# TensorE's instruction order inside an attention slot: row-maximum products behind the slot's other work, value products ahead of it

## The chip, the cores and the metric

The kernel runs on one core of a Trainium2 chip. The metric is the device time in microseconds of one execution; lower is better. The five engines of the core (TensorE, VectorE, ScalarE, GpSimd, SyncE) each run their own instruction list in order and meet only at semaphores.

## The reference

Input is x with 16 sequences of 256 rows and 128 columns. One transformer layer is computed, with 16 heads of 8 columns and 14 experts:

```
qkv = x @ w_qkv ; q, k, v split into 16 heads of 8
scores = q k^T / sqrt(8), causal
out = softmax(scores) @ v
a = layernorm(out @ w_proj + b_proj + x) * gamma + beta
x = layernorm(x + a)
logits = x @ gate_w.T ; the two best of 14 experts, softmax weights
h = gelu(x @ w1[e] + b1[e]) @ w2[e] + b2[e]
x = layernorm(x + clip(x + w_a h_a + w_b h_b, -100, 100))
```

## The kernel before

The program has three stretches. The first, up to about 300 us, is attention with everything that the routing needs, in a software pipeline over slots t = 0 to 21. The second runs the experts on tiles of 128 rows, the first of them already inside the last slots. The third gathers, adds, normalises and stores. The change lies in the first.

A slot t works on several sequences at once, each at another stage: sequence t is transposed and projected (`turn_x`, `project`, the value projection), t-2 gets its row maxima (`maxima` on TensorE, `reduce` on VectorE), t-3 and t-4 get scores, exponentials and value products (`scores`, `values`), t-4 its head normalisation and output projection, t-5 its layer norms and gate, t-6 its ranks and the scatter of its rows. Every slot has eight units u = 0 to 7, and all five engines run the same units, each in the order in which the Python body writes them. No planner moves anything: the order of TensorE's queue is the order of the `if` blocks in its `body`.

Names that matter:

- `maxima(t, r, i)`, i = 0 to 5: a first pass of score products of sequence t-2 into the PSUM tile M (both banks of it), with masks (L1506, L1512). It waits until VectorE has read M for the piece before (`m_reduced`).
- `reduce(i)` on VectorE (L1202): the maxima of one such piece, M into `row_max`. M is a single buffer, so `maxima(i+1)` and `reduce(i)` exclude each other.
- `scores` (L1473, masks L1481) into S[0] or S[1]; ScalarE's exponentials of it (L862) into `probs`.
- `values(t, r, s, k)`, k = 0 to 3 (L1531): probabilities times values of four heads into O, at u = 2, 3 (of t-4) and u = 5, 7 (of t-3).
- `heads_t` copies on ScalarE (L896 after u = 3, L938 after u = 7), `turn_heads` (L1539), then on VectorE `invert_sums` and `normalise_heads` (L1211, L1217).
- `split` on VectorE (L1034), then `m_split` on ScalarE (L882): remainders of the projected rows, for the three bf16 parts. ScalarE issues L882 ahead of L896.
- At u = 6 the transposes `x2T` (L1707) into M[0], which wait until all six reductions of the slot are done, and `on_turned` (L1712). At u = 7 the turn of the row maxima (L1609) into M[1], the gate (L1615) into M[0], the output projection (L1681), and the small product `shift_left` (L1688), which waits for ScalarE's copy L920.
- VectorE at the end of the slot: top two experts (MAX8 L1315, L1318, L1320), `y` (L1327), `both` (L1332); the next slot begins with the statistics of y (L1227) and `reduce(0)`.
- GpSimd scatters the rows of t-6 in units 2 to 5 (L775), from t = 6 on.

The core of VectorE's queue in a slot is: statistics of y, reduce(0), reduce(1), reduce(2), `ys`, `split`, reduce(3), statistics of ys, reduce(4), reduce(5), head normalisation, gate work.

Of the kernel before, what the change touches and what calls it, by code (L numbers as in the profile page):

```python
# [13 lines left out]
P = 128  # L14
# [12 lines left out]
def transformer_layer(nc, x, w_qkv, w_proj, b_proj, ln_gamma, ln_beta, gate_w, w1, b1, w2, b2, out):  # L27
# [49 lines left out]
    def on(s):  # L77

        return not isinstance(s, int) or 0 <= s < B
# [12 lines left out]
    with ExitStack() as ctx:  # L92
# [891 lines left out]
        def _(dve):  # L984
# [182 lines left out]
            def body(t, r, lap):  # L1167
# [128 lines left out]
                reduce(4)  # L1296
                if on(t - 4):
                    invert_sums(0)
                if on(t - 4):
                    normalise_heads(0)  # L1300
                steps(t, 4)
                reduce(5)
                if on(t - 4):
                    invert_sums(1)
                if on(t - 4):
                    normalise_heads(1)
                if t == B + 1:
                    first_list()
# [148 lines left out]
        def _(pe):  # L1457
# [139 lines left out]
            def body(t, r, lap):  # L1597
                for u in range(NP):
# [13 lines left out]
                    if u == 7 and on(t - 5):  # L1612
                        pe.wait_ge(x2T_copied, t - 4)
                        for i in range(TT):
                            last = pe.matmul(M[0][:, T + i * E:T + i * E + E], x2T[:, (r - 5) % R, i * P:i * P + P], gate_t[:, :],  # L1615
                                             start=True, stop=True)
                        last.then_inc(gate_ready, 1)
# [36 lines left out]
                    if u < NM and on(t - 2):  # L1654
                        maxima(t, r, u)
# [19 lines left out]
                    if u == 5 and on(t - 4):  # L1675
                        pe.wait_ge(o_normed, 2 * (t - 4) + 1)
                        turn_heads(t, 1)
                    if u == 7 and on(t - 4):
# [11 lines left out]
                    if pv_quad(t, u) and on(pv_quad(t, u)[0]):  # L1690
                        if u == 2 and on(t - 6):

                            pe.wait_ge(rank_read, t - 5)
                            if t == B + 1:
                                pe.wait_ge(first_table, 1)
                        if u == 5 and on(t):

                            pe.wait_ge(v_copied, t + 1)
                        values(t, r, *pv_quad(t, u))
# [9 lines left out]
                    if u == 6 and on(t - 4):  # L1709
                        pe.wait_ge(o_normed, 2 * (t - 3))  # L1710
                        for i in range(TT):
                            last = pe.transpose(G[:, i * P:i * P + P], heads[:, i], ident[:, :])  # L1712
                        last.then_inc(on_turned, 1)
                    if t == FIRST and u == 2:
# [88 lines left out]
```

## Time and profile before

| what | value |
|---|---|
| median of 3 runs | 504.61 us (498.4 to 506.06) |
| the profiled execution | 504.69 us |
| its span in the trace | 502.9 us |
| granted TensorE clock, mean | 0.886 |
| busy: TensorE, VectorE, GpSimd, ScalarE | 379.2, 325.1, 290.3, 266.8 us |
| reductions of the row maxima (L1202) | 96, the first at 16.7 us, the last at 280.0 us |

The time is that of the core's whole execution; the span is what the trace covers of it. Busy times are sums over instructions of an engine, so an engine can be the bound of one stretch and idle in another. Times in rows are us from the start of the span.

### The profile page before, as it was taken

To read this page: it belongs to the slowest core of one execution; us is meant where nothing else is said; L and a number is where in the kernel's file an instruction comes from. 1 tells how busy PE (TensorE), PEld (TensorE's weight loads), DVE (VectorE), ACT (ScalarE), POOL (GpSimd) and SP (SyncE) were. 2 spreads that over 40 slices of the span, in tenths; PEclk is the share of its full clock that TensorE was granted. 3 is DMA by queue.
4 is the path that set the end of the run, shared out by engine and by line. 5 is a ranking of instruction groups with operands and counts; after the bars stand their busy time and mean duration, and the time that the engine had idled before them with its cause. 6 is when DMAs were issued, how large, how long until landed. Compare 5 with 4: busy or idle time off the path is not lost. (4 is left out here: it accounts for less than half of the span.)

```text
span 502.9 us, 12961 instructions
## 1 busy us (share of the span) xinstructions
PE 379.2 (75%) x4207; PEld 276.0 (55%) x4207; DVE 325.1 (65%) x1053; ACT 266.8 (53%) x624; POOL 290.3 (58%) x454
## 2 busy tenths in 40 slices
PE   5477988977988798879877867765577877777780
PEld 3244555655555555556544435765466867756580
DVE  6634687758777877786786846734444776663386
ACT  2124666756776577666645637443346544444054
POOL 6402346775777668666754365785554555556271
PEclk9556999989999899998989869978787989798996
DMA  5412333334334433442311141222332222220573
GB/s 137 106 52 65 85 101 98 103 87 110 101 91 107 110 84 90 118 113 66 89 50 55 42 68 28 64 69 63 94 108 67 70 69 75 71 69 21 169 230 105
DMA packets 72974, 44.02 MB, mean 88 GB/s; under 512 B 13233, under 2 KB 68931, under 8 KB 72796
## 3 DMA queue, kind: packets, MB, share of 16 engines
q1 hardware_dynamic: 66650, 33.11, 25.0%
q0 software_dynamic: 4640, 9.36, 5.7%
q10 hardware_dynamic: 1618, 0.73, 0.6%
q8 instruction: 34, 0.56, 0.5%
q14 instruction: 32, 0.26, 0.2%
HBM read 18.54 MB, written 12.36 MB: 61 GB/s over the span
## 5 line engine op out<-in xcount | busy, mean ns | idle before, releaser
L1202 DVE TENSOR_REDUCE row_max<-M 128x4 f32<-128x1024 f32 (+1 forms) x96 | 117.2, 1221 | 48.8 <-PE M L1512 37.3
L862 ACT ACTIVATE probs<-S 128x768 f32<-128x768 f32 x128 | 102.7, 816 | 58.3 <-PE S L1481 42.5
L729 POOL DMA_INDIRECT results<-tile_rows x77 | 77.2, 1002 | 57.0 <-DVE tile_rows L1074 37.4
L775 POOL DMA_INDIRECT sorted_rows<-x,row_no x64 | 65.7, 1027 | 33.5 <-DVE row_no L1234 21.0
L1506 PE MATMUL M<-k_stack,q_stack 64*128 64x128 bf16 (+1 forms) x512 | 41.7, 267 | 43.4 <-DVE row_max L1202 40.3
L1531 PE MATMUL O<-probs,diag 128*32 128x256 f32 (+1 forms) x1024 | 58.5, 349 | 3.1 <-DVE row_chosen L1251 3.1
L748 POOL TENSOR_SCALAR_AFFINE_SELECT probs<-probs 128x256 f32<-128x256 f32 x104 | 40.0, 409 | 23.3 <-ACT probs L862 23.2
L1506 PEld LDWEIGHTS M<-k_stack,q_stack 64*128 64x128 bf16 x512 | 16.7, 100 | 62.6 <-DVE row_max L1202 57.0
L1473 PE MATMUL S<-q_stack,k_stack 64*128 64x256 bf16 (+1 forms) x512 | 45.6, 260 | 0.0
L1531 PEld LDWEIGHTS O<-probs,diag 128*32 128x32 f32 x1024 | 27.7, 113 | 25.4 <-issue 9.3
L852 ACT ACTIVATE hT<-S,q_stack 128x128 f32<-128x128 f32 x78 | 25.7, 371 | 25.0 <-PE S L1577 16.0
L782 POOL TENSOR_TENSOR diag<-rest,diag 128x512 bf16<-128x512 f32 x16 | 18.5, 1155 | 35.5 <-ACT diag L882 24.7
L852 ACT ACTIVATE hT<-S,k_stack 128x128 f32<-128x128 f32 x76 | 24.8, 371 | 20.5 <-PE S L1577 9.7
L1577 PE MATMUL S<-rows_t,k_stack 128*128 128x128 f32 x152 | 28.3, 318 | 7.7 <-ACT hT L852 4.4
L1512 PE MATMUL M<-ident_fold,mask_m 64*128 64x128 bf16 (+1 forms) x384 | 33.1, 255 | 0.0
L1577 PE MATMUL S<-rows_t,q_stack 128*128 128x128 f32 x156 | 27.1, 301 | 4.4 <-issue 2.7
L1577 PEld LDWEIGHTS S<-rows_t,k_stack 128*128 128x128 f32 x152 | 24.7, 231 | 8.9 <-issue 8.9
L1584 PE MATMUL M<-k_stack,hT 128*128 128x128 f32 x132 | 24.5, 317 | 4.1 <-DVE tile_rows L1074 3.5
L1473 PEld LDWEIGHTS S<-q_stack,k_stack 64*128 64x128 bf16 x512 | 16.6, 97 | 19.4 <-issue 17.1
L1065 DVE COPY q_stack<-experts 128x642 f32 x39 | 21.7, 559 | 8.0 <-issue 5.0
L1577 PEld LDWEIGHTS S<-rows_t,q_stack 128*128 128x128 f32 x156 | 23.4, 215 | 5.4 <-issue 5.3
L1584 PE MATMUL M<-q_stack,hT 128*128 128x128 f32 x116 | 21.9, 319 | 5.1 <-DVE tile_rows L1074 5.0
(261 smaller groups left out, 861.5 us busy)
## 6 DMA issues: line engine op xcount, KB each, us to landing
q_stack<-diag SPq DMA_DIRECT2D x96, 64.0 KB
k_stack<-diag SPq DMA_DIRECT2D x85, 64.0 KB
tile_rows<-sorted_rows SPq DMA_DIRECT2D x77, 64.5 KB
experts<-in_L_ffn_w_dram SPq DMA_DIRECT2D x28, 128.0 KB
xin<-in_L_attn_target_dram SPq DMA_DIRECT2D x16, 128.0 KB, 3.0
xres<-in_L_attn_target_dram SPq DMA_DIRECT2D x16, 128.0 KB, 3.1
out_dram<-probs SPq DMA_DIRECT2D x8, 256.0 KB, 2.3
q_stack<-results SPq DMA_DIRECT2D x7, 256.0 KB, 3.2
```

Of the source, the lines that this page charges most:

```text
L729: pool.indirect_dma_start(results, bass.IndirectOffsetOnAxis(ap=y_rows[:, slot, D:ROW].bitcast(U32), axis=0), y_rows[:, slot, 0:D], None, ...
L748: last = pool.affine_select(out=diag, in_=diag, compare_op=ALU.is_ge, fill=0.0, base=0, pattern=[[0, 2], [1, P]], channel_multiplier=-1)
L775: pool.indirect_dma_start(sorted_rows, bass.IndirectOffsetOnAxis(ap=row_no[:, q * 2 * TT + n:q * 2 * TT + n + 1], axis=0), x2[:, q, n % 2, ...
L852: act.activation(hT[:, (s - 2) % HR, f], hidden_of(s - 2, f), ACT.Gelu, bias=expert_now[(s - 2) % XR][:, AT_B1 + f:AT_B1 + f + 1]).then_in ...
L862: act.activation(probs[:, n].rearrange("p (a q) -> p a q", a=2), S[n % 2][:, :].rearrange("p (a q) -> p a q", a=2)[:, :, 0:T + P], ACT.Exp ...
L1202: dve.tensor_reduce(row_max[:, (r - 2) % R, :, g0:g0 + ng, half], M_both[:, :].rearrange("p (a h k) -> p a h k", a=2, h=ng), X, ALU.max).t ...
L1473: last = pe.matmul(S[n % 2][:, 512 * a + at:512 * a + at + nq], k_stack[rows, b, n, half * P:half * P + P], q_stack[rows, b, n, T - nq:T], ...
L1506: pe.matmul(M[a][:, j * keys:j * keys + keys], q_stack[rows, b, g0 + j, half * P:half * P + P], k_stack[rows, b, g0 + j, 0:keys], start=(j ...
L1512: last = pe.matmul(diag, mask_m[rows, c], ident_fold[rows, None, :].broadcast_to([TILE, ng, TILE]), start=False, stop=(c == 1), skip_group ...
L1531: last = pe.matmul(O[32 * j:32 * j + 32, at + T - nq:at + T], v_aug[:, b, half, h], probs[:, h // 2, (h % 2) * (T + P) + of:(h % 2) * (T + ...
L1577: pe.matmul(hidden_of(s - 2, f), expert_now[(s - 2) % XR][:, f * P:f * P + P], rows_t[:, (s - 2) % HR], start=True, stop=True).then_inc(h_ ...
L1584: last = pe.matmul(second(s - 4), hT[:, (s - 4) % HR, f], expert_now[(s - 4) % XR][:, AT_W2 + f * D:AT_W2 + f * D + D], start=(f == 0), st ...
```

## The change

On TensorE, three things move inside a unit. `maxima(t, r, u)` for u = 0 to 5 goes from the middle of the unit to its end: behind the projection (u = 2), the turns of the heads and the value projection (u = 4), the second turn (u = 5) and `values`. `values` goes ahead of the output projection, `shift_left`, the gate and the u = 6 transposes; at u = 7 it now stands directly behind the turn of the row maxima. The gate goes from ahead of all this to behind `values`. On VectorE, reduce(4) and reduce(5) each move behind one half of the head normalisation, so that VectorE's order fits TensorE's. No instruction is added or removed, and sizes, buffers and DMAs stay.

```diff
@@ VectorE's body @@
                 steps(t, 3)
-                reduce(4)
                 if on(t - 4):
                     invert_sums(0)
                 if on(t - 4):
                     normalise_heads(0)
+                reduce(4)
                 steps(t, 4)
-                reduce(5)
                 if on(t - 4):
                     invert_sums(1)
                 if on(t - 4):
                     normalise_heads(1)
+                reduce(5)
@@ TensorE's body @@
                         last.then_inc(shift_turned, 1)
-                    if u == 7 and on(t - 5):
-                        pe.wait_ge(x2T_copied, t - 4)
-                        for i in range(TT):
-                            last = pe.matmul(M[0][:, T + i * E:T + i * E + E], x2T[:, (r - 5) % R, i * P:i * P + P], gate_t[:, :],
-                                             start=True, stop=True)
-                        last.then_inc(gate_ready, 1)
...
                         turn_x(t, r, lap)
-                    if u < NM and on(t - 2):
-                        maxima(t, r, u)
...
                         turn_heads(t, 1)
+                    if pv_quad(t, u) and on(pv_quad(t, u)[0]):
+                        if u == 2 and on(t - 6):
+                            pe.wait_ge(rank_read, t - 5)
+                            if t == B + 1:
+                                pe.wait_ge(first_table, 1)
+                        if u == 5 and on(t):
+                            pe.wait_ge(v_copied, t + 1)
+                        values(t, r, *pv_quad(t, u))
+                    if u == 7 and on(t - 5):
+                        pe.wait_ge(x2T_copied, t - 4)
+                        for i in range(TT):
+                            last = pe.matmul(M[0][:, T + i * E:T + i * E + E], x2T[:, (r - 5) % R, i * P:i * P + P], gate_t[:, :],
+                                             start=True, stop=True)
+                        last.then_inc(gate_ready, 1)
...
-                    if pv_quad(t, u) and on(pv_quad(t, u)[0]):
-                        if u == 2 and on(t - 6):
-                            pe.wait_ge(rank_read, t - 5)
-                            if t == B + 1:
-                                pe.wait_ge(first_table, 1)
-                        if u == 5 and on(t):
-                            pe.wait_ge(v_copied, t + 1)
-                        values(t, r, *pv_quad(t, u))
...
                         last.then_inc(on_turned, 1)
+                    if u < NM and on(t - 2):
+                        maxima(t, r, u)
```

## Rows read from the trace of the kernel before

**Rows 1.** The page's groups by line: reductions, products for maxima; busy, mean, idle before.

```profile
L1202 DVE TENSOR_REDUCE row_max<-M 128x4 f32<-128x1024 f32 (+1 forms) x96 | 117.2, 1221 | 48.8 <-PE M L1512 37.3
...
L1506 PE MATMUL M<-k_stack,q_stack 64*128 64x128 bf16 (+1 forms) x512 | 41.7, 267 | 43.4 <-DVE row_max L1202 40.3
```

**Rows 2.** Windows: slot 5; slots 6 to 15; slot 13; slot 14. Columns: length, busy by engine, clock.

```profile
64.71:80.06 15.35, 13.90 (x209) 8.96 (x207) 12.22 (x32) 11.41 (x24) 7.89 (x17) 1.00 0.35 95
80.06:251.68 171.62, 146.00 (x2082) 94.70 (x2077) 127.44 (x354) 114.53 (x222) 121.53 (x220) 0.96 0.36 99
198.93:215.83 16.90, 13.99 (x213) 9.04 (x209) 12.64 (x36) 11.39 (x24) 12.15 (x23) 1.00 0.37 102
215.83:235.33 19.50, 16.68 (x213) 10.80 (x209) 12.75 (x36) 11.48 (x24) 12.60 (x24) 0.82 0.33 88
```

**Rows 3.** Timeline of slot 13, first half: start, length, engine, line, idle before.

```profile
198.93 1.22 DVE L1202 TENSOR_REDUCE row_max<-M 128x4 f32<-128x1024 f32 x1 [0.24 <-PE M L1512]
...
200.21 0.39 PE L1506 MATMUL M<-k_stack,q_stack 64*128 64x256 bf16 x4 [0.58 <-DVE row_max L1202]
...
200.92 1.13 PE L1558 MATMUL G<-diag,wqk 128*128 128x256 f32 x4
...
202.58 0.86 PE L1531 MATMUL O<-probs,diag 128*32 128x256 f32 x16
202.69 1.22 DVE L1202 TENSOR_REDUCE row_max<-M 128x8 f32<-128x1024 f32 x1
...
203.37 0.34 PE L1473 MATMUL S<-q_stack,k_stack 64*128 64x256 bf16 x4
...
204.20 0.28 PE L1512 MATMUL M<-ident_fold,mask_m 64*128 64x128 bf16 x4
...
204.36 0.68 DVE L1034 TENSOR_TENSOR rest<-G,diag 128x512 f32<-128x512 f32 x1
...
205.07 0.62 ACT L882 CAST diag<-rest 128x512 bf16<-128x512 f32 x1 [0.23 <-issue]
...
206.47 1.23 DVE L1202 TENSOR_REDUCE row_max<-M 128x4 f32<-128x1024 f32 x1 [1.43 <-remote]
206.63 0.59 ACT L896 COPY heads_t<-O 128x512 f32<-128x512 f32 x1 [0.94 <-PE O L1531]
...
207.75 0.39 PE L1506 MATMUL M<-k_stack,q_stack 64*128 64x256 bf16 x4 [2.10 <-DVE row_max L1202]
```

**Rows 4.** Timeline of the same slot, second half.

```profile
208.18 0.66 PE L1539 MATMUL G<-ident,heads_t 128*128 128x128 f32 x4
...
209.22 0.34 PE L1473 MATMUL S<-q_stack,k_stack 64*128 64x256 bf16 x4
...
209.63 0.40 PE L1506 MATMUL M<-k_stack,q_stack 64*128 64x128 bf16 x8
...
210.18 0.66 PE L1539 MATMUL G<-ident,heads_t 128*128 128x128 f32 x4
210.29 1.23 DVE L1202 TENSOR_REDUCE row_max<-M 128x8 f32<-128x1024 f32 x1 [0.23 <-PE M L1512]
...
210.76 0.86 PE L1531 MATMUL O<-probs,diag 128*32 128x256 f32 x16
...
211.82 0.44 PE L1707 MATMUL M<-ident,x 128*128 128x128 f32 x2
...
213.06 0.62 PE L1615 MATMUL M<-gate_t,x2T 128*128 128x14 f32 x4
...
213.71 0.26 DVE L1315 MAX8 top_v_all<-M 128x8 f32<-128x14 f32 x2 [1.71 <-PE M L1615]
...
215.10 0.49 DVE L1227 BATCH_NORM_STATS2 stats<-y 128x6 f32<-128x128 f32 x2
```

**Rows 5.** Timeline of slot 5 on VectorE: its third and fourth reductions, no scatter yet.

```profile
68.48 1.22 DVE L1202 TENSOR_REDUCE row_max<-M 128x8 f32<-128x1024 f32 x1 [0.19 <-PE M L1512]
...
70.75 1.21 DVE L1202 TENSOR_REDUCE row_max<-M 128x4 f32<-128x1024 f32 x1
```

## The prediction

> **What bounds the kernel now.** I read the page's groups first. The largest is VectorE's reduction of the row maxima, 96 times 1.22 us; TensorE in turn stands idle 43.4 us ahead of the products that fill M for it, nearly all of it on those reductions [rows 1]. That is 0.45 us per piece and 2.7 us per slot, and it is TensorE's largest wait in the page's groups. So the slot is a shuttle between two engines over one buffer: products, reduction, products. Whatever TensorE is given between two pieces is free up to the 1.22 us of the reduction and is paid beyond it.
>
> The windows say how tight this is. Slot 13 lasts 16.90 us, with TensorE busy 13.99 and VectorE 12.64 [rows 2]. Slots 6 to 15 average 17.16 us at a clock of 0.96. Slot 14, at 0.82, took 19.50: 2.6 more than slot 13 for 0.18 of clock, so 0.04 costs an estimated 0.6 and an average slot at full clock 16.56 us. Slot 5, the last without the scatters of GpSimd (7.89 us busy there against 12.15), took 15.35 [rows 2].
>
> The timeline shows where that difference sits. In slot 13 the products of the fourth piece end at 204.48, and VectorE is free at 205.04, but the reduction starts at 206.47, released late; ScalarE gets the end of the value products only at 206.63; TensorE's next products then stand until 207.75, idle 2.10 [rows 3]. In slot 5 the fourth reduction follows the third after 2.27 us without any wait [rows 5]; in slot 13 after 3.78 [rows 3]. So 1.43 us of a slot goes to a TensorE signal that arrives late near the scatters. Why it is late, these rows don't show.
>
> **The change, as gaps.** No work is added. What changes is what lies between `maxima(i)` and `maxima(i+1)`. Behind piece 0: two scores, rank, turn, as before. Behind piece 1: scores and projection, and now also the values of u = 2. Behind 2: scores and values, as before. Behind 3: scores, the turn of the heads and the value projection, in place of values and scores. Behind 4: scores, second turn, values. Behind 5: one scores, and then the x2T transposes, which need that last reduction. Before, a turn, values and a scores covered it. One gap becomes too full, one empty, and one now hangs on ScalarE.
>
> **One slot walked.** Zero is the start of the products of piece 5 (209.63 before). Distances are between starts in slot 13.
>
> 1. The reduction starts 0.66 later and takes 1.23 [rows 4]; VectorE's end reaches TensorE in 0.06 (200.15 to 200.21 [rows 3]). x2T starts at 1.95. Before it was 2.19, with a turn and values inside [rows 4]; now TensorE idles about 1.1.
> 2. From x2T to the gate it was 1.24 [rows 4]. The values now stand ahead of the gate, 0.79 (202.58 to 203.37 [rows 3]): gate at 3.98. No cover exists for this: VectorE already waits 1.71 for the gate [rows 4].
> 3. Gate to MAX8 0.65, MAX8 to the end of the statistics of y 1.88 [rows 4]: next slot's reduction 0 at 6.51, before at 6.20 (215.83 [rows 2]). Plus 0.31. `shift_left` and its copies on ScalarE come later too, behind values, gate and projection, but TensorE reaches them near 5.2, and `maxima(0)` needs them only about 5.9, so I cost that at nothing; if ScalarE is later than that, it is paid in full.
> 4. Reduction 0 to projection 1.99; the projection 1.13, values 0.79 [rows 3], then `maxima(2)` and 0.66: reduction 2 at 11.08. That is 4.57 after reduction 0, before 3.76 [rows 3]. Plus 0.81.
> 5. Reduction 2 to the end of `split` 2.35, to the end of ScalarE's `m_split` (L882) 3.00, then the copy of the heads (L896) 0.59 [rows 3] and a hand-over at either end: turn of the heads at 14.8. In the old order `maxima(4)` stood ahead of this turn; now it stands behind it, and behind the value projection, 1.04 together [rows 4]: `maxima(4)` at 15.8. Counted from reduction 0 that is 9.3, before 8.82 (198.93 to 207.75 [rows 3]). This is plus 0.48 in all for steps 4 and 5, although the old 8.82 holds the 1.43 of the late signal. What was lost to lateness is now lost to a chain VectorE, ScalarE, TensorE.
> 6. `maxima(4)` 0.43 [rows 3, 4], scores 0.41, second turn 0.58, values 0.79 [rows 3, 4]: `maxima(5)` at 18.02. Before 1.88 for this, now 2.21: plus 0.33. The head normalisation moved ahead of the reduction on VectorE is hidden under the products.
>
> The slot is 18.02 against 16.90, plus 1.12. One term is soft: TensorE's own end is modelled, and behind a 1.13 us projection the next issue may come 0.2 earlier; I take 17.8. Against the full-clock average of 16.56 that is plus 1.25 (bounds 0.9 and 1.5).
>
> The late signal is the unknown. Its old end was 7.54 after reduction 0; at the same distance it would be 14.05, just where ScalarE is free for the copy, so it costs nothing. That is one end. The other is that it follows the products: `maxima(3)` would end at 12.9, and 1.99 later (204.48 to 206.47 [rows 3]) is 14.9, which moves the copy by 0.8 to 0.9 per slot. It could also vanish, and below nothing it can't go, since the chain of step 5 stands without it. I take nothing, as the scatters are issued by GpSimd's clock and not by TensorE's.
>
> **The sum.** Slots 6 to 15: 10 x 1.25 = 12.5. Slot 5 has the same chains and no lateness to trade, 17.8 minus 15.35 [rows 2]: 2.5. Slots 16 and 17 have no projection, split or value projection; steps 1 to 3 and half of 6 remain, about 0.5 each (0 to 1): 1.0. Slots 2 to 4 have neither gate nor x2T and partly a clock at half speed; 0.8 once for step 4 (0 to 2). Slots from 18 on have no maxima; the gate of slot 18 is later by one values, which the waiting experts' list may hide. Together 16.8. The expert and output stretches keep their length and start that much later. The profiled execution took 504.69, which is the median (504.61): 504.7 + 16.8 = 521.5, rounded to 522.
>
> **A rule that speaks for no change.** In slot 13 VectorE is busy 12.64 of 16.90 us, TensorE's weight loads 9.04 [rows 2]. The Trainium skill, page "Perfetto Trace Analysis", section "Identifying the Most-Contended Engine", says to take occupancy for VectorE and the busy share of weight loads for TensorE, and to improve the engine that is highest. By that rule VectorE is the bound and TensorE's order would be nearly free: about 505. The trace does not agree fully, because VectorE itself waits 1.43 and 1.71 us in the slot for TensorE [rows 3, 4].
>
> **The rivals.**
>
> - *VectorE is the bound* (0.14). VectorE has 12.64 us of work per slot and slack of 4.3; the later gate and projection come out of slack if the chain through L882 overlaps with something I laid end to end. Without step 5's wait on ScalarE, TensorE could turn the heads at about 13.3 instead of 14.8, and the slot is 16.3 to 16.6, as before: 505, with a few us either way. For it: the idle shares. Against it: L896 stands behind L882 in ScalarE's queue, and L882 behind `split`.
> - *The waits get covered* (0.08), the faster side. Values issued ahead of a piece run while the reduction does, and the 2.7 us of idle per slot [rows 1] shrink. Its price is bounded by slot 5's 15.35: ten slots at 17.16 minus 15.35 give 18 us, half of it 9, so 495. It decides if TensorE's turn of the heads isn't waiting, that is, if the copy L896 lands before the scores of u = 4 are issued. In slot 13 it ends at 207.22, held by the late signal [rows 3]; now it would be held by L882.
> - *The clock* (0.16), beyond the forecast. About 3.8 us of TensorE's slot would now be idle, in three lumps of 0.7 to 1.5. Slot 14, partly at the 1.2 GHz level (mean 0.82), shows the price: 2.6 more than slot 13 [rows 2]. If two in three of slots 5 to 15 get such a stretch or half of one more than now, 8 to 12 us come on top: 531.
>
> **How the numbers follow.** The forecast has 0.62 and its own range is 514 to 530: bounds 0.9 and 1.5 per slot, with part of the lateness at the top. Below it lie the rivals at 505 and 495, above it 531. To leave out no more than 2 in 10, the range is 505 to 533. A change under 2% (10 us) can hardly be told from none here, given runs from 498.4 to 506.06. Faster by over 2% takes most of the second rival: 0.06. Within 2%: the first rival, the rest of the second and the lowest part of the forecast: 0.18. Slower: 0.76.
>
> **What would show it.** Right: slots of 17.5 to 18.3 us at full clock; x2T (L1707) idle about 1.1 on L1202; MAX8 waiting some 2.5; L1539's first turn waiting over 1 us for L896; reductions 0 and 2 about 4.6 apart instead of 3.76; the lateness ahead of reduction 3 gone from VectorE's idle. Wrong: slots at or under 16.9, or L896 landing ahead of the scores of u = 4; then step 5 failed. If slots are near 18.7 or more, the late signal followed the products or the clock fell more often; the granted clock of the ten slots (0.96 before) tells these two apart.

## The result, and the profile after

The changed kernel took 524.63 us (median of 4 runs, 522.45 to 527.59) against 504.13 (4 runs, 498.4 to 506.06): 20.5 us slower. The ratio is 1.0447 [1.0359 to 1.0535]; it counts only runs in the faster of the two states in which a kernel is found here, and so it isn't the quotient of the two medians. Its profiled execution took 523.96 us, with a span of 522.2 and a mean granted clock of 0.903 (before: span 502.9, clock 0.886). The span rose by 19.3.

First the busy times and the groups by line that answer to [rows 1].

```profile
PE 369.8 (71%) x4207; PEld 275.1 (53%) x4207; DVE 323.1 (62%) x1053; ACT 268.7 (51%) x624; POOL 289.7 (55%) x454
...
L1202 DVE TENSOR_REDUCE row_max<-M 128x4 f32<-128x1024 f32 (+1 forms) x96 | 117.3, 1221 | 60.0 <-PE M L1512 56.5
L1506 PE MATMUL M<-k_stack,q_stack 64*128 64x128 bf16 (+1 forms) x512 | 41.3, 264 | 26.5 <-DVE row_max L1202 19.0
...
L1539 PE MATMUL G<-ident,heads_t 128*128 128x128 f32 x128 | 24.4, 321 | 23.2 <-ACT heads_t L896 19.5
```

The work is the same: 96 reductions of 1221 ns. What changed is who waits for whom. TensorE's idle time ahead of the maxima products fell from 43.4 to 26.5 us [rows 1], which looks like a success. But VectorE's ahead of the reductions rose from 48.8 to 60.0, now nearly all on L1512, and three other waits grew. The turn of the heads waits 23.2 us, 19.5 of it for ScalarE's copy; the group had 2.0 before. The other two are the x2T transposes (before 5.2) and the first maximum behind the gate (before 33.1), in the grouped view by line:

```profile
L1705 PE MATMUL M<-ident,x 128*128 128x128 f32 x32 | 6.8, 296 | 24.9 <-issue 19.6 <-ACT x L907 4.1 <-DVE row_max L1202 1.2
L1315 DVE MAX8 top_v_all<-M 128x8 f32<-128x14 f32 x32 | 4.1, 170 | 41.1 <-PE M L1683 41.1
```

("issue" stands for a wait of x2T to which no releaser was found; in the timeline below it ends right behind the sixth reduction.) The windows that answer to [rows 2]: slots 2 to 4, slot 5, slots 6 to 15, slot 12, slot 13.

```profile
16.64:62.38 45.74, 31.50 (x411) 20.52 (x413) 25.75 (x29) 19.42 (x36) 13.47 (x25) 0.76 0.29 76
62.38:79.72 17.34, 13.39 (x211) 9.25 (x206) 12.34 (x33) 11.37 (x22) 7.86 (x17) 1.00 0.32 84
79.72:268.00 188.28, 143.65 (x2082) 99.14 (x2076) 126.56 (x355) 116.89 (x222) 121.36 (x220) 0.95 0.33 90
192.99:211.37 18.38, 13.61 (x214) 9.35 (x209) 12.53 (x36) 11.68 (x23) 12.12 (x22) 1.00 0.34 93
211.37:230.41 19.04, 15.09 (x214) 10.56 (x209) 12.66 (x36) 11.60 (x23) 12.12 (x22) 0.91 0.33 89
```

Slots 6 to 15 went from 171.62 us [rows 2] to 188.28, at almost the same clock (0.96, now 0.95). So the loss is no matter of the clock. It lies in the slots that the change speaks of. The ledger, from the starts of reductions in both traces (before: slots 2 to 4 took 48.02 us, at a clock of 0.69):

| stretch | before | after | change | predicted |
|---|---|---|---|---|
| slots 2 to 4 | 48.02 | 45.74 | -2.3 | +0.8 |
| slot 5 | 15.35 | 17.34 | +2.0 | +2.5 |
| slots 6 to 15 | 171.62 | 188.28 | +16.7 | +12.5 |
| slots 16, 17, to the last reduction | 28.33 | 32.19 | +3.9 | +1.0 |
| all behind the last reduction | 222.89 | 222.01 | -0.9 | 0 |

The total came out at +19.3, near the 16.8 of the forecast, but partly because errors cancel. To see them, here is the timeline of slot 12 after, a slot at full clock (start, length, engine, line, idle before), which answers to [rows 3, 4].

```profile
192.99 1.21 DVE L1202 TENSOR_REDUCE row_max<-M 128x4 f32<-128x1024 f32 x1
...
197.47 1.23 DVE L1202 TENSOR_REDUCE row_max<-M 128x8 f32<-128x1024 f32 x1 [0.81 <-PE M L1512]
...
198.98 0.28 PE L1512 MATMUL M<-ident_fold,mask_m 64*128 64x128 bf16 x4
...
200.43 0.59 ACT L896 COPY heads_t<-O 128x512 f32<-128x512 f32 x1
200.53 1.23 DVE L1202 TENSOR_REDUCE row_max<-M 128x4 f32<-128x1024 f32 x1 [0.71 <-PE M L1512]
...
201.07 0.66 PE L1539 MATMUL G<-ident,heads_t 128*128 128x128 f32 x4 [1.54 <-ACT heads_t L896]
...
202.70 0.29 DVE L1217 TENSOR_TENSOR heads<-G,inv_sum 128x128 f32<-128x128 f32 x1
...
202.91 1.21 DVE L1202 TENSOR_REDUCE row_max<-M 128x4 f32<-128x1024 f32 x1
...
203.04 0.66 PE L1539 MATMUL G<-ident,heads_t 128*128 128x128 f32 x4 [0.27 <-DVE heads L1217]
...
204.42 0.40 PE L1506 MATMUL M<-k_stack,q_stack 64*128 64x128 bf16 x8
...
204.66 0.38 PE L1512 MATMUL M<-ident_fold,mask_m 64*128 64x256 bf16 x4
...
205.79 1.22 DVE L1202 TENSOR_REDUCE row_max<-M 128x8 f32<-128x1024 f32 x1 [1.18 <-PE M L1512]
...
207.11 0.41 PE L1705 MATMUL M<-ident,x 128*128 128x128 f32 x2 [1.91 <-issue]
```

Three things are to be seen. The third reduction starts 4.48 behind the first (before 3.76). The turn of the heads waits 1.54 for L896. And two reductions start late for no work that the trace shows: the fourth piece's masks end at 198.98 + 0.28 = 199.26, its reduction starts at 200.53, after VectorE has idled 0.71; the sixth's masks end at 205.04, its reduction starts at 205.79, and x2T behind it has idled 1.91 instead of 1.1. The prediction took it that the first lateness would cost nothing, and had no second one. In between VectorE never waits: the fifth reduction follows half of the head normalisation (L1217) directly, and the second turn of the heads waits for that half.

For all ten slots, in each of which six reductions mark the time, the distances between their starts (0 to 1, 1 to 2, and so on, the last to the next slot's first), as means over the slots that ran at full clock throughout:

| kernel | such slots | slot | 0-1 | 1-2 | 2-3 | 3-4 | 4-5 | 5-0 | others, mean |
|---|---|---|---|---|---|---|---|---|---|
| before | 7 | 16.47 | 1.83 | 1.94 | 3.20 | 1.95 | 1.95 | 5.60 | 18.78 |
| after | 5 | 18.57 | 1.81 | 2.67 | 3.21 | 2.44 | 2.87 | 5.58 | 19.08 |

### The profile page after: what moved, and what is told of

Its sections match the earlier page's. It is cut to its first block and busy times, and to the rows that moved or that the text cites. A ratio compares the mean times of both kernels' runs of the same rounds, so it can differ in the third digit from the quotient of the medians.

```text
span 522.2 us, 12961 instructions
## 1 busy us (share of the span) xinstructions
PE 369.8 (71%) x4207; PEld 275.1 (53%) x4207; DVE 323.1 (62%) x1053; ACT 268.7 (51%) x624; POOL 289.7 (55%) x454
## 5 line engine op out<-in xcount | busy, mean ns | idle before, releaser
L1202 DVE TENSOR_REDUCE row_max<-M 128x4 f32<-128x1024 f32 (+1 forms) x96 | 117.3, 1221 | 60.0 <-PE M L1512 56.5
L1531 PE MATMUL O<-probs,diag 128*32 128x256 f32 (+1 forms) x1024 | 60.8, 346 | 2.6 <-DVE row_chosen L1251 2.6
L1506 PE MATMUL M<-k_stack,q_stack 64*128 64x128 bf16 (+1 forms) x512 | 41.3, 264 | 26.5 <-DVE row_max L1202 19.0
L1531 PEld LDWEIGHTS O<-probs,diag 128*32 128x32 f32 x1024 | 30.9, 113 | 24.1 <-issue 9.7
L782 POOL TENSOR_TENSOR diag<-rest,diag 128x512 bf16<-128x512 f32 x16 | 18.5, 1155 | 43.4 <-ACT diag L882 25.4
L1506 PEld LDWEIGHTS M<-k_stack,q_stack 64*128 64x128 bf16 x512 | 15.6, 97 | 48.5 <-DVE row_max L1202 27.4
L1539 PE MATMUL G<-ident,heads_t 128*128 128x128 f32 x128 | 24.4, 321 | 23.2 <-ACT heads_t L896 19.5
L1512 PE MATMUL M<-ident_fold,mask_m 64*128 64x128 bf16 (+1 forms) x384 | 32.8, 252 | 0.0
L1539 PEld LDWEIGHTS G<-ident,heads_t 128*128 128x128 f32 x128 | 15.7, 159 | 29.7 <-ACT heads_t L896 21.9
L1315 DVE MAX8 top_v_all<-M 128x8 f32<-128x14 f32 x32 | 4.1, 170 | 41.1 <-PE M L1683 41.1
L1577 PE MATMUL S<-rows_t,k_stack 128*128 128x128 f32 x152 | 24.9, 289 | 3.9 <-issue 3.8
L1584 PEld LDWEIGHTS M<-k_stack,hT 128*128 128x128 f32 x132 | 19.6, 213 | 12.5 <-issue 9.9
```

The source lines that it names most:

```text
L1202: dve.tensor_reduce(row_max[:, (r - 2) % R, :, g0:g0 + ng, half], M_both[:, :].rearrange("p (a h k) -> p a h k", a=2, h=ng), X, ALU.max).t ...
L1506: pe.matmul(M[a][:, j * keys:j * keys + keys], q_stack[rows, b, g0 + j, half * P:half * P + P], k_stack[rows, b, g0 + j, 0:keys], start=(j ...
L1531: last = pe.matmul(O[32 * j:32 * j + 32, at + T - nq:at + T], v_aug[:, b, half, h], probs[:, h // 2, (h % 2) * (T + P) + of:(h % 2) * (T + ...
L1539: last = pe.transpose(G[:, k * P:k * P + P], heads_t[:, k, i * P:i * P + P], ident[:, :])
L1577: pe.matmul(hidden_of(s - 2, f), expert_now[(s - 2) % XR][:, f * P:f * P + P], rows_t[:, (s - 2) % HR], start=True, stop=True).then_inc(h_ ...
L1584: last = pe.matmul(second(s - 4), hT[:, (s - 4) % HR, f], expert_now[(s - 4) % XR][:, AT_W2 + f * D:AT_W2 + f * D + D], start=(f == 0), st ...
```

## The experiments

My theory behind the result: the loss is a sum of gaps of TensorE that became longer than a reduction (pieces counted from 0: values ahead of piece 2, the chain through L882 and L896 ahead of piece 4, values ahead of piece 5), with VectorE and TensorE shuttling over M. The rivals: VectorE alone is the bound, or the lateness of TensorE's signals makes the loss. Twelve kernels were run, two of them the kernels before and after once more. Four undo a part of the change; where they ran, the kernel before took 502.0 (497.57 to 506.31, 7 runs), so by its times this is the chip of the comparison above, called the first chip here. The other eight happened to run on another chip, where the kernel before takes 448 to 450 us; each is compared only with before on its own chip, and the times in us that were forecast for four of them (those with moved scatters and old_u2_moved), meant for the first chip, can't be compared.

### One part undone at a time

**u5_back**: the sixth piece goes back ahead of the second turn and the values.

```diff
+                    if u in (5,) and on(t - 2):
+                        maxima(t, r, u)          # behind turn_x, ahead of turns and values
...
-                    if u < NM and on(t - 2):
+                    if u < NM and u not in (5,) and on(t - 2):
                         maxima(t, r, u)          # at the unit's end
@@ VectorE @@
+                reduce(5)
                 if on(t - 4):
                     invert_sums(1)
                 if on(t - 4):
                     normalise_heads(1)
-                reduce(5)
```

> The changed kernel with one piece undone: in unit 5 the products for the sixth piece stand again ahead of the second turn of the heads and the values, and VectorE reduces that piece ahead of the second half of the head normalisation. Theory (a shuttle over one buffer; step 1 and step 6 of the prediction): the x2T transposes are covered again, their idle of 1.91 us falls under 0.8, and the slot gets 0.4 us shorter if the signal of the sixth piece stays 0.7 late, 0.9 if it does not: 514 to 520. Rival (the slot is held elsewhere, by the chain through ScalarE's two copies, and TensorE only waits in another place): within 2 us of the changed kernel, 523 to 526.

Measured: 521.3 us (516.88 to 525.9), ratio to before 1.0381 [1.0265 to 1.0496]. The forecast of 514 to 520 was missed by 1.3, and by the times alone the gain over the changed kernel isn't clear of the intervals. Slots at full clock took 18.12 (7 of them), with 2.14 from 4 to 5 in place of 2.87 and 5.91 from 5 to 0 in place of 5.58. So the step gives 0.73 in one place and takes 0.33 back in the other; with hundredths elsewhere 0.46 per slot is left. Most of the 0.73 is the sixth piece's late signal: in six of the seven slots its reduction now starts 0.04 to 0.20 behind the masks, where it was 0.49 to 0.86 in the full-clock slots of the changed kernel. In the view by line x2T's idle shrinks from 24.9 to:

```profile
L1707 PE MATMUL M<-ident,x 128*128 128x128 f32 x32 | 7.5, 319 | 5.0 <-ACT x L907 4.5 <-issue 0.5
```

The gap behind the sixth piece was empty in the changed order; filled again, it holds a turn and values that cost no more than the 0.33.

**u7_back**: the gate goes back ahead of the values at u = 7, and the values behind `shift_left`.

```diff
+                    if u == 7 and on(t - 5):
+                        pe.wait_ge(x2T_copied, t - 4)
+                        ...                      # gate, directly behind the turn of the row maxima
...
-                    if pv_quad(t, u) and on(pv_quad(t, u)[0]):
+                    if u != 7 and pv_quad(t, u) and on(pv_quad(t, u)[0]):
...
+                    if u == 7 and on(t - 3):
+                        values(t, r, *pv_quad(t, u))   # behind shift_left
```

> The changed kernel with one piece undone: in unit 7 the gate stands again directly behind the turn of the row maxima and the values come last. Theory (step 2 and 3): VectorE's MAX8 waits about 0.8 us less (2.6 to 1.8), but the next slot's first reduction then waits for its products as in the kernel before, so a slot gains only 0.2 to 0.3 us: 520 to 523. Rival (the gate alone sets the slot's end): the full 0.79 us of the values per slot comes back, 12 slots, 514 to 516.

Measured: 526.09 (524.45 to 530.22), 1.0552 [1.0455 to 1.0649], no faster than the changed kernel as far as the intervals tell; the forecast of 520 to 523 was missed. The slots at full clock (five, one of them at 0.99) took 18.35 in place of 18.57, with 5.28 from 5 to 0 in place of 5.58, about the 0.2 to 0.3 that was expected per slot; other slots hide it (five with a stretch at the lower clock level, mean 19.23). By the time this run is inconclusive; by the distances step 3 is right in sign and small.

**u2_back**: the third piece goes back ahead of projection and values (the diff is that of the first, with `(2,)` and without the VectorE part).

> The changed kernel with one piece undone: in unit 2 the products for the third piece stand again ahead of the values. Theory (step 4 and 5, a chain from the third reduction over split, L882 and L896 to the turn of the heads): the first and third reduction are 3.7 to 3.8 us apart again instead of 4.5, everything behind them moves up by 0.7 to 0.8, 12 slots: 514 to 517. Rival (the late TensorE signal of unit 3 holds L896, whatever split does): the reductions move up but L896 still starts when the signal of the values arrives, gain under 0.3 us per slot: 521 to 525.

Measured: 529.87 (524.05 to 546.93, 5 runs), 1.0525 [1.0408 to 1.0643]. The 514 to 517 of the theory did not come. The profiled execution is the longest of the five (546.93, mean clock 0.849), and each of its slots 6 to 15 has a stretch at the lower clock, so only what lies ahead of such a stretch is read. In slot 9 it is 3.77 again from reduction 0 to 2, but 3.94 from 2 to 3; together 7.71, the same as after (7.69). The masks end at 150.62 there, and the fourth reduction starts at 152.21. In slot 5 of the same trace, at full clock and without a late signal, the earlier third piece does buy 0.73 (16.61 against 17.34). So the rival of lateness is the better reading here, though it rests on one trace.

**u45_back**: fifth and sixth pieces back ahead of the turns (as in the first diff with `(4, 5)`, and both reductions ahead of their halves of the head normalisation).

> The changed kernel with units 4 and 5 undone on TensorE and VectorE: both pieces stand again ahead of turns, value projection and values, and both reductions ahead of the head normalisation. Theory (step 5 and 6): the products of the fifth piece go out as soon as the fourth reduction is done, the turn of the heads follows 0.4 us later, the sixth piece leaves 0.7 us earlier and x2T another 0.5: a slot 1.0 to 1.4 us shorter, 507 to 513. Rival (ScalarE's copy L896 stays the release and the products ahead of the turn only delay it): within 3 us of the changed kernel.

Measured: 515.56 (513.88 to 518.8), 1.0335 [1.025 to 1.0421], with 507 to 513 forecast. The one slot at full clock took 17.66, 0.9 less than after, with 1.91 and 1.91 for 3 to 4 and 4 to 5: both steps gone. But the ten slots took 186.71, hardly less than 188.28, and their window says why:

```profile
80.17:266.88 186.71, 151.59 (x2082) 101.67 (x2076) 126.48 (x356) 115.09 (x222) 122.01 (x220) 0.92 0.33 91
```

The clock is 0.92 in place of 0.95: nine slots of ten have a stretch at 1.2 GHz. With the nine at 17.66 the ten slots would be 10 us shorter (an estimate), so in this kernel the clock took back most of what the order gave inside them: the prediction's third rival at work, in a place where it wasn't looked for. It also means that only 1.6 of the 10 us between the two traces lie in these slots; 5.2 lie in slots 16 and 17 (26.99 against 32.19) and 3.8 behind the last reduction (218.23 against 222.01).

### A chip without late signals

The next two were made to move the lateness: GpSimd's scatters were taken out of units 2 to 5, since slot 5 [rows 5] had been without both.

```diff
-            return ... if t >= B + 4 else {2: (0,), 3: (1,), 4: (2,), 5: (3,)}.get(u, ())
+            return ... if t >= B + 4 else {6: (0, 1), 7: (2, 3)}.get(u, ())
```

They ran on the second chip, with before at 448.06 (446.86 to 448.51, 7 runs). **old_scatter_late** is the kernel before with this edit, **new_scatter_late** the changed one with it.

> The kernel before with one thing moved: GpSimd issues the four scatters of a slot in units 6 and 7 instead of 2 to 5. Nothing else. Theory (the late TensorE signal of unit 3 comes with the scatters): the fourth reduction starts right behind split, the third and fourth reduction are 2.3 us apart instead of 3.2 in slots at full clock, and those slots go from 16.47 to about 15.5: 10 slots, 490 to 497. Rival (the lateness comes with the 64 KB transfers of the projected parts or with TensorE itself): the distance stays at 3.2 and the time within 3 us of the kernel before.

> The changed kernel with the same move of the scatters to units 6 and 7. Theory (scatters make the signals late): the third and fourth reduction come to 2.4 apart (the walk of the prediction without lateness), the sixth piece's signal is on time, a slot at full clock falls from 18.6 to 17.6 or 17.8 as walked: 510 to 516. Rival (transfers or TensorE itself): 3.2 stays, 522 to 526.

Measured: 465.37, 1.0434 [1.0365 to 1.0503], and 470.68, 1.0517 [1.0492 to 1.0542]. The first is an experiment that failed: it brought a wait of its own. The late scatters hold up the small work that GpSimd does for VectorE, `rstd` (L767): in slot 12 it starts 5.5 behind the first reduction (186.53), in the unedited kernel on the same chip 2.1. VectorE in a slot of **old_scatter_late**:

```profile
184.80 1.22 DVE L1202 TENSOR_REDUCE row_max<-M 128x8 f32<-128x1024 f32 x1
...
187.29 0.62 DVE L1280 SCALAR_TENSOR_TENSOR ys<-yg,rstd,x_beta 128x128 f32<-128x128 f32 x2 [1.27 <-POOL rstd L767]
...
188.43 1.21 DVE L1202 TENSOR_REDUCE row_max<-M 128x4 f32<-128x1024 f32 x1
```

From reduction 2 to 3 that is 3.63, where the unedited kernel takes 2.26 on this chip (below). So it told nothing of the late signals. What told it was the chip itself, with the two kernels as they are, run again as **old_again** and **new_again** (before: 449.75, 445.32 to 452.12, 13 runs).

> The kernel before itself, for a trace from the same chip as the three that follow. If the late TensorE signals belong to the program, slots 6 to 15 show 3.0 to 3.8 us between third and fourth reduction at full clock, as in the first trace, and a slot of about 16.5. If they belong to the chip on which a program runs, a chip without them shows 2.3 and a slot near slot 5's 15.35.

> The changed kernel itself on the same chip. On a chip with late signals: a ratio of 1.04 to 1.05, slots of 18.4 to 18.8 at full clock. On one without: slots of 17.3 (as with the scatters moved), 1.9 more than the old order's 15.35, 12 slots, 20 to 24 us slower, a ratio near 1.05 against some 448 us.

Measured: 449.88 for the first; 470.77 (469.12 to 472.07), 1.0509 [1.0421 to 1.0597], for the second. Their ten slots, before and then changed:

```profile
78.11:232.57 154.46, 140.28 (x2082) 90.59 (x2076) 126.11 (x355) 113.43 (x222) 121.19 (x220) 1.00 0.41 110
```

```profile
79.09:253.82 174.73, 137.22 (x2082) 94.48 (x2076) 126.85 (x355) 115.57 (x222) 121.27 (x220) 0.99 0.36 97
```

Here the clock is full, but for one stretch in slot 14 of new_again, no signal is late, and each slot is like the others to 0.01 us, but for slots 10 and 15 of old_again and 14 and 15 of new_again (15.66 and 15.77, 18.78 and 17.77):

| kernel, second chip | typical slot | 0-1 | 1-2 | 2-3 | 3-4 | 4-5 | 5-0 |
|---|---|---|---|---|---|---|---|
| old_again | 15.38 | 1.83 | 1.94 | 2.26 | 1.90 | 1.91 | 5.54 |
| new_again | 17.27 | 1.81 | 2.67 | 2.26 | 2.85 | 2.09 | 5.58 |

The change costs 1.89 per slot with all lateness away: 0.73 for step 4, 0.95 for step 5, 0.18 for step 6, 0.04 for steps 1 to 3. So the loss needs no lateness: it comes whole without it. **new_scatter_late** has the distances of new_again, so in the changed order the later scatters hold nobody up. The reductions of a slot of old_again, and ScalarE's copy between them:

```profile
172.48 1.22 DVE L1202 TENSOR_REDUCE row_max<-M 128x4 f32<-128x1024 f32 x1 [0.24 <-PE M L1512]
...
174.42 1.23 DVE L1202 TENSOR_REDUCE row_max<-M 128x8 f32<-128x1024 f32 x1
...
176.69 1.22 DVE L1202 TENSOR_REDUCE row_max<-M 128x4 f32<-128x1024 f32 x1
...
177.33 0.58 ACT L896 COPY heads_t<-O 128x512 f32<-128x512 f32 x1
...
178.59 1.19 DVE L1202 TENSOR_REDUCE row_max<-M 128x4 f32<-128x1024 f32 x1
...
180.50 1.22 DVE L1202 TENSOR_REDUCE row_max<-M 128x8 f32<-128x1024 f32 x1 [0.23 <-PE M L1512]
```

And of new_again:

```profile
187.21 1.22 DVE L1202 TENSOR_REDUCE row_max<-M 128x8 f32<-128x1024 f32 x1 [0.81 <-PE M L1512]
...
188.87 0.68 DVE L1034 TENSOR_TENSOR rest<-G,diag 128x512 f32<-128x512 f32 x1
...
189.47 1.21 DVE L1202 TENSOR_REDUCE row_max<-M 128x4 f32<-128x1024 f32 x1
189.59 0.62 ACT L882 CAST diag<-rest 128x512 bf16<-128x512 f32 x1 [1.29 <-DVE rest L1034]
190.11 0.58 ACT L896 COPY heads_t<-O 128x512 f32<-128x512 f32 x1
...
190.74 0.66 PE L1539 MATMUL G<-ident,heads_t 128*128 128x128 f32 x4 [1.48 <-ACT heads_t L896]
...
191.78 0.39 PE L1506 MATMUL M<-k_stack,q_stack 64*128 64x256 bf16 x4
...
192.33 1.23 DVE L1202 TENSOR_REDUCE row_max<-M 128x4 f32<-128x1024 f32 x1 [0.30 <-PE M L1512]
...
193.75 0.40 PE L1506 MATMUL M<-k_stack,q_stack 64*128 64x128 bf16 x8
...
194.41 1.22 DVE L1202 TENSOR_REDUCE row_max<-M 128x8 f32<-128x1024 f32 x1 [0.37 <-PE M L1512]
...
195.74 0.41 PE L1705 MATMUL M<-ident,x 128*128 128x128 f32 x2 [1.20 <-issue]
```

The lower list shows the chain of step 5 link by link, `split` (L1034), L882, L896, L1539; in the upper one the same copy ends at 177.91, before the fifth reduction begins, and nobody waits.

### The parts by themselves, without lateness

**old_u2_moved** is the kernel before with step 4 alone: the third piece goes behind the values.

```diff
-                    if u < NM and on(t - 2):
+                    if u < NM and u != 2 and on(t - 2):
                         maxima(t, r, u)
...
                         values(t, r, *pv_quad(t, u))
+                    if u == 2 and on(t - 2):
+                        maxima(t, r, u)
```

> The kernel before with one part of the change alone: in unit 2 the products for the third piece go out behind the values. Theory (step 4 alone): the second and third reduction are 2.67 apart instead of 1.94; of these 0.73 most is given back ahead of the fourth, because the late signal or split ends last there, but the values and scores of unit 3 go out later too: 0.3 to 0.7 per slot, 506 to 511. Rival (gap 1 is the cost of the whole change): 0.73 or more per slot stays and the clock falls more often, 514 or more. Second rival (the late signal swallows it whole): 500 to 504.

Measured: 457.89, 1.0191 [1.0131 to 1.0251]; the ratio makes 8.6 us. The typical slot is 16.11. Two reductions of it:

```profile
179.18 1.23 DVE L1202 TENSOR_REDUCE row_max<-M 128x4 f32<-128x1024 f32 x1 [0.24 <-PE M L1512]
181.85 1.22 DVE L1202 TENSOR_REDUCE row_max<-M 128x8 f32<-128x1024 f32 x1 [0.81 <-PE M L1512]
```

2.67 instead of 1.94, with the other distances unchanged: ten slots by 0.73 are 7.3 us, and one stretch at the lower clock adds 1.3 (a slot of 17.42). The forecast let most of the 0.73 be given back ahead of the fourth reduction; without a late signal to wait for, none was. The same step that u2_back could not show in slots 6 to 15 of the first chip is there in full, and it is TensorE's order alone.

**new_heads_first** and **new_scatter_late_heads_first** test step 5. In the changed kernel ScalarE copies the heads ahead of its share of `split` (the first on the changed kernel, the second on new_scatter_late).

```diff
@@ ScalarE @@
+                    if u == 3 and on(t - 4):
+                        act.wait_ge(pv_done, 4 * (t - 3))
+                        ...                      # copy O to heads_t
                     ...                          # m_split, the cast of the remainders
-                    if u == 3 and on(t - 4):
-                        act.wait_ge(pv_done, 4 * (t - 3))
-                        ...
```

> The changed kernel with the scatters in units 6 and 7, and ScalarE copying the heads (L896) ahead of the remainder cast (L882) in unit 3. Theory (step 5: the turn of the heads waits for L896 behind L882 behind split): with the signals on time and the copy first, the first turn of the heads goes out when split is done, 0.9 to 1.2 us earlier than with the scatters moved alone, 12 slots: 498 to 505. Rival (the copy's place does not matter, the values' end or the exponential ahead of it holds it): within 3 us of the changed kernel with the scatters moved.

> The changed kernel with ScalarE's copy of the heads (L896) ahead of its remainder cast (L882), scatters in their old place. Theory (step 5, the chain through L882 and L896): without late signals the fourth and fifth reduction come 0.45 closer, 12 slots, 5 to 7 us less than the changed kernel; with late signals L896 starts when the values' signal arrives, which was as late as L882's end, and nothing is gained. Rival: the copy's place never matters, within 2 us on either chip.

Measured: 463.67, 1.0362 [1.0338 to 1.0386], and 464.82, 1.0375 [1.0287 to 1.0463]; 7.0 and 6.0 us less than their counterparts. From reduction 3 to 4 it is 2.37 (before this edit 2.85), from 4 to 5 it is 2.17 (2.09), and the typical slot takes 16.87 (17.27); six slots of new_heads_first take 17.0 to 17.15, most of it from 4 to 5. In new_heads_first, where the copy is L885:

```profile
185.39 0.59 ACT L885 COPY heads_t<-O 128x512 f32<-128x512 f32 x1
...
186.80 0.63 PE L1539 MATMUL G<-ident,heads_t 128*128 128x128 f32 x4 [0.43 <-DVE rest L1034]
...
189.08 0.66 PE L1539 MATMUL G<-ident,heads_t 128*128 128x128 f32 x4 [0.57 <-DVE heads L1217]
```

The turn no longer waits for ScalarE; it waits for `split` itself, and the second turn for the head normalisation. So half of step 5's 0.95 hung on the order of two copies in ScalarE's queue. The other half stays with the turn and the value projection, which now stand ahead of the piece, and with the wait for `split`; no run parts these.

**old_scores_ahead** asks whether the old order leaves anything: the scores of u = 2 go from behind the second reduction to ahead of it, where they could hide in the reduction's 1.22 us.

```diff
-                    if on(s):
+                    if on(s) and not (u == 2 and t < B + 2):
...
+                    if u == 1 and t < B + 2 and on(t - 3):
+                        scores(t, r, *s_unit(t, 2))
```

> The kernel before with one move of another kind: the scores of unit 2 go out at the end of unit 1's other work, ahead of the products for the second piece, where TensorE idles 0.58 us for the first reduction. Theory (the shuttle: what fits under a reduction is free): 0.3 to 0.37 us of scores is hidden there and the third piece's products no longer wait behind it, 0.2 to 0.35 us less per slot, 12 slots: 2 to 4 us faster than the kernel before. Rival (VectorE's queue sets the first three reductions): no change within 1 us.

Measured: 449.94 (10 runs), 1.0032 [0.9999 to 1.0065], and the same distances as old_again. The hope of a gain fell: the old order's distances 0 to 1 and 1 to 2 are already the 1.22 of the reduction, 0.06 for its signal and 0.54 or 0.66 for the products. Moved work was hidden before. No run gave a version that beats the kernel before.

## Why the prediction was right, and which terms were off

The forecast case came: slower, 524.6 where 522 was said, by 20.5 us where 17.4 was said. Of the signs that it named, x2T's idle time (1.20 without lateness, 1.91 with it), MAX8's wait (2.58, in slot 12 of both traces of the changed kernel), the turn's wait for L896 (1.54) and the distance between reductions 0 and 2 (4.48) came. Two did not: the slot at full clock took 18.57, above 17.5 to 18.3, and the lateness ahead of reduction 3 stayed. Step by step, with new_again for the steps as walked, since it holds no lateness:

- **Steps 1 and 2.** x2T 1.99 behind the products of the sixth piece, idle 1.20 (walked 1.95 and 1.1); from there to the gate 1.82 (2.03). The late values do delay the gate.
- **Step 3.** 6.25 from these products to the next slot's first reduction (6.51). Over before, that is 0.04 instead of 0.31 (5.58 against 5.54 between the reductions). u7_back, with the gate back ahead, has 5.28, so the values cost about 0.3 there, and the earlier x2T gives about as much back; the walk had counted too much for the first.
- **Step 4.** 4.49 between reductions 0 and 2 (4.57), +0.73 per slot. old_u2_moved shows it alone.
- **Step 5.** From reduction 2 to `split`'s end 2.34, to the end of L882 3.00, to the turn 3.53 (2.35, 3.00, 3.72), idle 1.48 on L896. The chain is as walked; new_heads_first cuts it.
- **Step 6.** 1.97 from the fifth piece's products to the sixth's (2.21).

The steps make 17.27 where 18.02 was walked and 17.8 taken: right in kind, 0.5 too long. The term that was mis-sized, and which the prediction put at nothing, is the **late signal**. On the first chip the slot after was 18.57, 1.3 above the same program's 17.27 without lateness; before, it was 16.47 against 15.38, 1.1. Against its base of 16.56 the full-clock slot rose by 2.0, against the 16.47 by 2.1, not by 1.25. The prediction had taken the late moment as fixed by GpSimd's clock, at the same distance from reduction 0. It moved with the products: over the slots at full clock the fourth reduction came 6.97 behind reduction 0 before and 7.69 after, 0.72 later, as the third piece did.

Slot 12 of the changed kernel on the two chips shows where this is paid (times behind the slot's first reduction). The fourth reduction starts at 7.54 against 6.75. The first turn of the heads starts at 8.08 against 8.02, since the copy is held by L882 on both: up to here the lateness costs almost nothing, as predicted. But VectorE is late by it. Step 6 called the head normalisation ahead of the reduction hidden under the products; it is in new_again, where the fifth reduction waits 0.30 for its products, and not here, where that reduction comes straight from VectorE's queue at 9.92 against 9.61. The second turn waits for the same head normalisation, the products of the sixth piece start at 11.43 against 11.03, and the sixth reduction, with its own late signal, at 12.80 against 11.69. So of 1.11 us 0.40 came back through VectorE's queue, and 0.71 is the second late signal, for which the sum had no term.

Three other terms were off, and one of them hid much of this. The **stretches at the lower clock**: a slot that had one cost 2.3 more before (18.78 against 16.47), but after only 0.5 (19.08 against 18.57). That isn't because TensorE's new idle time hides it: the one such slot of new_again cost 1.5 more (18.78 against 17.27). In the five such slots after, the sixth reduction starts 0.04 behind its masks, so the second late signal is missing there. Ten slots: 10 x 2.10 = 21.0, less 3 x 2.31 that before had paid, plus 5 x 0.51, make 16.6, the ledger's 16.7 but for rounding; that these means add up says nothing on the causes. Slots 2 to 4 came out 2.3 shorter instead of 0.8 longer, at a clock of 0.76 instead of 0.69. Slots 16 and 17 rose by 3.9 instead of 1.0, at 0.89 instead of 0.94. In each of them the sixth reduction comes 4.28 behind the fifth, where it was 1.91 before and is 2.17 in new_again; in slot 16:

```profile
279.52 0.64 PE L1512 MATMUL M<-ident_fold,mask_m 64*128 64x256 bf16 x4
...
281.24 1.23 DVE L1202 TENSOR_REDUCE row_max<-M 128x8 f32<-128x1024 f32 x1 [2.58 <-PE M L1512]
```

Of the 2.1 above new_again, 1.1 is again a late signal, from the masks' end at 280.16 to 281.24. The other 1.0 goes with a stretch at the lower clock, in which the values took 1.51 in place of 0.86. On the second chip these two slots fell from 26.59 to 25.97 while the clock there rose from 0.87 to 1.00:

```profile
232.57:259.16 26.59, 21.50 (x333) 13.62 (x332) 20.70 (x57) 14.63 (x26) 13.20 (x25) 0.87 0.18 52
```

```profile
253.82:279.79 25.97, 19.90 (x360) 13.80 (x359) 21.09 (x58) 15.86 (x27) 13.90 (x25) 1.00 0.19 54
```

So nothing there can be put down to the order with certainty.

That the total lies within 3 us of the forecast is in part luck: the steps were taken 0.5 too long per slot and 1.3 of lateness was left out; of what this adds to slots 6 to 15 the stretches at the lower clock took about half away (21.0 became 16.6), and slots 2 to 4 took away what slots 16 and 17 added.

The rivals. **VectorE is the bound** fell: its busy time hardly changed (325.1 to 323.1) and its idle time grew. The rule of the Trainium skill, page "Perfetto Trace Analysis", section "Identifying the Most-Contended Engine", would have named it, with 12.64 busy of 16.90 us [rows 2]; by its measure VectorE was the highest. Yet old_u2_moved, with one piece moved in TensorE's order alone, costs 1.9%: no engine's share shows a shuttle over one buffer. **The waits get covered** fell with step 5: the copy doesn't land in time. **The clock** hardly fell in this kernel (0.96 to 0.95 over slots 6 to 15, with stretches in five of them in place of three), but took most of u45_back's gain in these slots.

What stays open: why TensorE's signal arrives late. It goes with the chip: the same programs, scatters included, show it in slots 6 to 15 of the first chip and not in these slots on the second. On the first chip slot 5, the last without scatters, hasn't got it either; whether the scatters are needed for it there was not tested, since both kernels with moved scatters ran on the second. Nor do the traces tell a late signal from late products, as the ends of TensorE's instructions are modelled. And why the sixth piece's lateness is missing in the slots with a stretch at the lower clock, and nearly so in u5_back, no run shows.

## What to carry to other kernels

Where two engines share a single buffer, read the distances between starts of the reader: what the writer does between two pieces is free up to the reader's length (here 1.22 us) and paid beyond it: 0.79 us of values in a gap already full cost 0.73. Before work is moved ahead of a hand-over, look in the other engines' queues for what its input stands behind: half of the worst step here was two copies in the wrong order on ScalarE. A delay that only the timeline shows should be followed through the queue of every engine it touches: here it was absorbed on the way to TensorE's turn and came back through VectorE's. And an estimate of the pure steps is best made on slots at full clock.

## What the runs showed of the hardware

- **Late signals of TensorE.** Masks that end at 199.26 release VectorE only at 200.53, though it had idled 0.71 by then, and the second of the slot is 0.75 late (205.04 to 205.79). Behind most other pieces the reduction starts 0.04 us behind the masks' end. In new_again, the same program on another chip, the sixth reduction starts at 194.41, 0.66 behind the start of its products, and the fourth directly behind `split`.
- **Two chips.** One kernel takes 502 to 504 us on one and 448 to 450 on the other. In the traces slots 6 to 15 hold 17 us of it (171.62 against 154.46) and the part behind the last reduction 34 (222.89 against 188.94), the latter at clocks of 0.86 and 0.91:

```profile
259.16:448.10 188.94, 143.31 (x1152) 122.22 (x1152) 127.06 (x539) 104.53 (x316) 124.03 (x144) 0.91 0.35 98
```

- **Stretches at 1.2 GHz.** Of slots 6 to 15, every second one of the changed kernel got one, beginning 8.1 to 8.5 us behind the slot's first reduction, near the first turn of the heads, ahead of which TensorE had idled 1.5 to 1.9 us; the slots at full clock have the same idle time. Before, three had one, in u45_back nine. On the second chip none did in the kernel before and one in the changed kernel. So neither the program nor this idle time alone sets it.
